# Attention on a graph: one more wait ahead of GpSimd's gathers, on VectorE's query product three steps back

## The reference, cut to what matters

```python
Q = (x @ Wq + bq).reshape(n, H, DH)
K = (x @ Wk + bk).reshape(n, H, DH)
V = (x @ Wv + bv).reshape(n, H, DH)
score = jnp.sum(K[src] * Q[dst], axis=-1) / np.sqrt(DH)
score = jnp.exp(jnp.clip(score, -5.0, 5.0))
wV = jax.ops.segment_sum(V[src] * score[..., None], dst, num_segments=n)
z = jax.ops.segment_sum(score, dst, num_segments=n)
attn = (wV / (z[..., None] + 0.001)).reshape(n, D)
h = layer_norm(x + attn, gamma1, beta1)
h = h + jax.nn.relu(layer_norm(h, gamma2, beta2) @ Wo + bo)
```

## Time and profile before

| | us |
|---|---|
| median of 3 runs | 2628.74 |
| lowest, highest | 2619.01, 2636.85 |
| the profiled execution's own time | 2645.04 |
| its span, first to last instruction | 2639.7 |
| first to last gather of attention (starts) | 1244.9 to 2591.6 |
| GpSimd busy with the 808 gather instructions | 786.8 |
| VectorE's 202 query products | 139.3, idle 715.9 before them |

### The profile page before, as it was taken

One profiled execution on the slowest core, in us unless ns is written; L12 is line 12 of the kernel. 1 busy time (PEld: TensorE's weight loads), 2 busy tenths in 40 slices (PEclk: granted clock), 3 DMA queues, 4 the chain that ended last, 5 costly groups with the idle time before them and its releaser, 6 DMA issues.

```text
span 2639.7 us, 44819 instructions
## 1 busy us (share of the span) xinstructions
PE 1717.0 (65%) x10229; PEld 1152.3 (44%) x10229; DVE 1372.1 (52%) x3608; ACT 937.1 (35%) x2332; POOL 1180.4 (45%) x1458
## 2 busy tenths in 40 slices
PE   2666666898989999897445555555555555554454
PEld 0222223454556565564344444444444444443443
DVE  8888876335656333365344444444454444444444
ACT  2777764234644222121132232232232322322223
POOL 4444434123534100012656565556555565555551
PEclk9555555899999999998666676666666666667666
DMA  1000001001111110134333333333333333333331
GB/s 66 0 0 0 0 10 50 23 28 43 54 51 57 31 32 29 29 97 135 112 99 113 95 118 99 101 104 112 94 111 98 107 118 95 108 110 98 104 96 32
DMA packets 148865, 188.64 MB, mean 71 GB/s; under 512 B 25795, under 2 KB 117316, under 8 KB 148804
## 3 DMA queue, kind: packets, MB, share of 16 engines
q0 software_dynamic: 38784, 105.96, 13.9%
q1 hardware_dynamic: 110020, 82.00, 9.9%
HBM read 162.82 MB, written 25.04 MB: 71 GB/s over the span
## 4 chain that ended last, share of the span: by engine, by line
another core or an unknown queue 17%; DVE 12%; issue 11%; PE 11%; ACT 1%; DMA 0%; POOL 0%; DVEq 0%; ACTq 0%
PE acc_bank L1391 5%; PE aq_bank L1372 4%; DVE counts L1497 3%; DVE a_score L1500 3%; DVE counts L1505 1%; PE ap_bank L1378 1%; DVE counts L1429 1%; DVE a_clipped L1510 1%; PE ac_bank L1408 0%; PE ac_bank L1407 0%; DVE counts L1453 0%; DVE a_stat L1460 0%; POOL counts L1302 0%; DVE counts L1446 0%
## 5 line engine op out<-in xcount | busy, mean ns | idle before, releaser
L1302 POOL DMA_INDIRECT counts<-keys_values,a_index x808 | 786.8, 974 | 564.9 <-ACT a_index L1317 336.0
L813 PE MATMUL z_bank<-y_parts,counts 128*128 128x384 bf16 (+1 forms) x3750 | 666.5, 329 | 4.1 <-DMA y_parts<-in_L_gnn_bq 4.1
L1497 DVE TENSOR_TENSOR counts<-aq_bank,counts 128x512 f32<-128x512 f32 x202 | 139.3, 690 | 715.9 <-remote 511.5
L1391 PE MATMUL acc_bank<-counts 128*128 128x136 f32 x1616 | 347.4, 370 | 236.6 <-issue 132.7
L1372 PE MATMUL aq_bank<-counts 128*128 128x128 bf16 x2424 | 285.0, 263 | 329.6 <-issue 314.0
L813 PEld LDWEIGHTS z_bank<-y_parts,counts 128*128 (+1 forms) x3750 | 370.2, 99 | 239.0 <-issue 15.0
L1391 PEld LDWEIGHTS acc_bank<-counts 128*128 128x128 f32 x1616 | 293.4, 260 | 278.2 <-issue 152.5
L1372 PEld LDWEIGHTS aq_bank<-counts 128*128 128x128 bf16 x2424 | 212.0, 120 | 387.6 <-issue 378.6
L1333 ACT ACTIVATE counts<-a_clipped 128x32 f32<-128x32 f32 x202 | 46.1, 228 | 896.3 <-DVE a_clipped L1510 780.1
L381 POOL TENSOR_TENSOR key_low_build<-iota_b_build,src_cols_build 128x768 bf16<-128x768 bf16 x102 | 151.7, 1488 | 210.6 <-DVE flat_build L452 196.4
L469 DVE TENSOR_TENSOR counts<-share_build,counts 128x300 f32 x408 | 166.3, 468 | 42.1 <-PE share_build L533 40.8
(11 more groups left out here) (159 smaller groups left out, 2061.0 us busy)
## 6 DMA issues: line engine op xcount, KB each, us to landing
counts<-group_rel_rows SPq DMA_DIRECT2D x34, 768.0 KB
counts<-keys_values,a_index POOLq DMA_INDIRECT x808
self_term<-s_out SPq DMA_DIRECT2D x150, 64.0 KB, 1.6
s_in<-self_term SPq DMA_DIRECT2D x150, 64.0 KB, 1.8
residual<-x_in SPq DMA_DIRECT2D x75, 64.0 KB, 1.6
counts<-query_parts SPq DMA_DIRECT2D x34, 96.0 KB
x_in<-in_x SPq DMA_DIRECT2D x50, 64.0 KB, 1.8
x_in<-residual SPq DMA_DIRECT2D x50, 64.0 KB, 1.9
```

The costliest lines, as they stand in the source:

```text
L813: yield s, nc.tensor.matmul(bank(p, dt)[:, 0:width], counts[:, bass.ds(dt.value(P) + s * NA, P)], y3[(p - 1) % 2][:, s, 0:width], start=s ...
L1302: nc.gpsimd.indirect_dma_start(rows_kv[:, j, c, :], None, v.kv, bass.IndirectOffsetOnAxis(index[:, j, c:c + 1], 0)).then_inc(gathered[j], 16)
L1391: ins = nc.tensor.matmul(acc_bank[ga.slot()][:, 0:TW], pick[:, s2.slot(3), c, :], msg[:, s2.slot(3), c, :], start=j == 2 and c == 0, stop= ...
L1497: nc.vector.tensor_tensor(prod[:, :].rearrange("p (c d) -> p c d", c=GC), q_bank[s.slot()][:, :].rearrange("p (c d) -> p c d", c=GC), rows ...
```

## The change

Ahead of a step's four gathers GpSimd gets a third wait. Beside the row numbers and the free slot, gather s now waits for s-2 query products, which is for the product of step s-3. The two other waits stay. No instruction moves on any engine; each step from s = 3 on gets one wait (with the increment of `held` that follows each such wait). The first three steps have none.

```diff
     RG = GS
+    LEAD_OF_GATHERS = 3
     PAIR = 2 * GS
...
                 if sub(s):
                     (s + 1).count(pool, index_ready, held)
                     (s - (RG - 1)).count(pool, msg_done, held)
+                    (s - (LEAD_OF_GATHERS - 1)).count(pool, prod_done, held)
                     for c in range(GC):
                         nc.gpsimd.indirect_dma_start(rows_kv[:, j, c, :], None, v.kv,
                                                      bass.IndirectOffsetOnAxis(index[:, j, c:c + 1], 0)).then_inc(gathered[j], 16)
```

## The result

The changed kernel takes 2559.99 us (median of 4 runs, 2556.61 to 2563.45) against 2626.59 us of the kernel before: a ratio of 0.9718, 95% interval 0.9693 to 0.9743. It is faster by 2.8%, where 1% slower was forecast; rival A had put it at 2569 us.

What follows compares the result with a forecast made beforehand. No engine is full; an order of events paces attention's gathers, with TensorE slow while they run. Gathers +31 us and the end -6.5 give +25 us, taking the median of 2628.74 to 2654; range 2580 to 2700.

Steps and rivals of the forecast that it cites:

- rival A: Attention's gathers: the third product's matmuls still get out, so all cycles have three steps; -60 us, 2569 us; chance 0.18.
- Point 1: GpSimd's waits before each step's gathers: the new wait on product s-3 is always the last to end.
- Point 2: GpSimd's gathers: released by the product itself, a run starts at 1.67 us in place of 3.92, 2.25 us sooner.
- restart: VectorE: the first query product after a run of gathers; its start is the time T that the forecast counts from.
- Point 3: GpSimd: a run's first gather meets VectorE's message product and costs 0.25 us more a run, ends 0 and 0.5.
- Point 4: TensorE: the third product's query matmuls end 3.6 to 3.9 us into the run, past 3.3; most cycles pass only two.
- Point 5: Gather cycles: 14.25 us for two steps, 19.25 for three, 3 in 10 of three; 6.85 us a step.
- rival C: Attention's gathers: a third product never passes, 7.12 us a step in place of 6.67; +79 us, 2708 us; chance 0.15.
- Point 6: Gathered rows: with two or three products a cycle they are there at the restart, so their lateness costs nothing.
- Point 7: The sum: gathers 1378 us against 1346.7, +31; the stage's end 9.2 us in place of 15.7, -6.5; together +25.
- Rival B: TensorE isn't held by the gathers, so the shorter pause is pure gain; -124 us, 2505 us; chance 0.06.
- the crawl: TensorE's results come out very slowly from soon after a run of gathers starts until its last rows have landed.

Runs made afterwards that it cites:

- qd3_c: Changed kernel with GpSimd's third wait on TensorE's query matmuls of step s-3 in place of VectorE's product: 2510.45 us against 2638.71 for the kernel before (0.9530).
- late3: Changed kernel with GpSimd's third wait on ScalarE's copy of the selection of step s-3 in place of VectorE's product: 2618.15 us against 2625.32 before (0.9963).
- lead4_c: Changed kernel with the third wait on the product of step s-4 in place of s-3: 2560.7 us against 2638.71 for the kernel before (0.9715).
- few_long: Changed kernel plus 4 matmuls of 512 columns ahead of each step's query matmuls, written over by them: 2552.18 us, ratio 0.9714 to the kernel before.
- many_short: Changed kernel plus 12 matmuls of one column ahead of each step's query matmuls, written over by them: 2557.52 us, ratio 0.9746 to the kernel before.
- direct_c: Changed kernel with GpSimd issuing plain DMAs of 1 KB rows from fixed places in place of indirect gathers: 1942.61 us, kernel before at 2638.71.
- half_rows: Changed kernel with gathers of 512 bytes a row in place of 1 KB, wrong rows and no values: 2311 us in three sets.
- after2: The changed kernel itself, unaltered, run again in another set: 2322.76 us against 2326.15 for the kernel before (0.9983).

## Why the prediction was wrong

It was wrong at the fourth step ("what is late next"), and the price of the fifth was too high. The others stand:

- Point 1, the new wait is the last one: right. 221.7 us of the pauses, 73 times, end on the product.
- Point 2, the run starts 1.67 us after the restart: 1.50 measured, the median over the runs (3.92 before).
- Point 3, the first gather made longer by the message product: right, 1.33 us in the median where 1.2 to 1.5 was forecast. All gathers together became 33 us longer; 22 was reckoned, 0 to 44 were the ends. In qd3_c, whose run starts ahead of the message product, the first gather takes 0.94 us.
- Point 4: wrong. The third product's query matmuls were to end 3.6 to 3.9 us into the run, and so to be caught in seven cycles of ten. They ended at +4.03, later still, and were caught in hardly any: 54 of 59 third products came promptly. I took the limit as a time from the run's start (3.3 us, a few up to 4.3). The kernel before can't tell this from a limit counted from the restart, since its runs nearly all start at one distance from it. The changed kernel can: of all query matmuls that ended 3.5 to 5.5 us after the run's start, 5 of 48 had a prompt product before and 53 of 59 after.

The table has the third product of each cycle of two steps and more. Prompt means that it started within 1.5 us of the end of its query matmuls and of VectorE's instruction before it. Times are medians; the instructions are TensorE's matmuls and weight loads on record from the restart to the end of those query matmuls.

| | run's start after restart, us | query matmuls' end after restart, us | instructions | prompt |
|---|---|---|---|---|
| before | 3.92 | 5.54 | 52 | 57 of 58 |
| late3 | 3.66 | 5.55 | 57 | 57 of 57 |
| after | 1.50 | 5.53 | 66 | 54 of 59 |
| lead4_c | 1.50 | 5.53 | 66 | 56 of 56 |
| few_long | 1.50 | 6.98 | 88 | 39 of 64 |
| many_short | 1.50 | 5.85 | 104 | 26 of 65 |
| qd3_c | 0.77 | 5.53 | 59 | 17 of 71 |

In the first four the matmuls end at the same distance from the restart and pass, wherever the run starts from 1.50 us on. So moving the run from 3.92 to 1.50 us costs hardly a product. The last three rows forbid a general limit in time from the restart: many_short's end 0.3 us later and mostly fail, few_long's end later than those and pass more often, and qd3_c's end at the same 5.53 us and mostly fail. A number of instructions since the restart, some 90, would fit all rows but qd3_c's. So the step that failed is known; what the limit is counted in is not.

- Point 5: the price of a cycle of three was right, 19.25 us forecast and 19.01 measured in the mean. Against the kernel before this gains 1.2 us a cycle and not the whole 2.25 of point 2: before, these cycles ran from 17.6 to 21.3 us with a mean of 20.20, and I took one of 21.25 for all. The share was wrong with point 4: of 69 runs 42 have three steps, 13 have more and 6 have two, in place of seven in ten with two. And the price of a cycle of two was too high: 14.25 us forecast, 13.4 in the only two of the changed kernel, 12.2 in many_short and 12.1 in qd3_c. Part of it is the 3.60 us from the last gather to the restart, read from one cycle: the kernel before's median is 3.16. At 6.1 us a step even cycles of two would have been faster than the 6.67 before, so rival C's slowdown wasn't there either. The stage takes 6.30 us a step, 6.85 was forecast and 6.42 was rival A's.
- Point 6, the rows come in time: right, VectorE waited for rows 5 times, 9.3 us.
- Point 7: the end of the stage gave 11.5 us, 6.5 was reckoned. The last product starts 4.2 us after the last gather, where 9.2 was put.

Rival A is what happened: the third product passes and the pause is simply shorter. It forecast 60 us, and the medians show 69 from 2628.74. The range of 2580 to 2700 was said to take in most of A and of C, and left out the times of both, 2569 and 2708.

Rival B has a share too. It took a rule, that DMA never contends with a compute engine (the Trainium skill, SBUF — State Buffer, section Who interferes with whom), to mean that the gathers don't hold TensorE. In three sets of five they don't: the kernel before takes 2326 us and the gathers run without a pause. In the sets with the crawl B fails: between 2136 and 2140 TensorE started nothing, and its signal came when the rows had stopped. Whether that goes against the rule isn't shown. direct_c moved rows at 214 GB/s with no product held, which agrees with it; what holds TensorE needn't be the transfer of rows.

What stays open: what the crawl is, what sets its limit, and why a whole set of runs has it or not. The number of the chip isn't the reason: the first set, with the crawl, and the second, without it, both have chip 14 on record. One thing was seen and not explained: the three sets that held half_rows had no crawl, and the two sets and the first measurement that didn't hold it had it. That it was about chance was my expectation before the fifth set; with that set it is six out of six, and no run tests it apart.

## What to carry to other kernels

Where an engine stops and restarts in cycles, ask for every threshold what it is counted from: a time from the one event, from the other, or a number of instructions. A trace with one rhythm can't tell them apart, and a forecast across the change then rests on a choice; look for a second kernel or stage in which they lie at different distances. Look at the cycles beside the time: two kernels with the same time (the changed one and many_short) had quite different ones. With the crawl it paid to release the long-running queue (GpSimd's gathers here) from the earliest event of the cycle that proves progress: by way of ScalarE 2618 to 2639 us, by VectorE's product 2560, by TensorE's matmuls 2510. Without the crawl it gives next to nothing: the kernel before takes 2326 and those by way of VectorE or TensorE 2323. And measure the kernel before beside each trial: here it moved by 300 us between sets, over four times what the change gains.

## What the runs showed of the hardware

The same kernel takes 2625 to 2639 us in some sets of runs and 2326 us in others, within 1% inside each. The difference is in the stage with indirect gathers: the changed kernel takes 237 us less in after2, and its gathers' starts span 1040.7 us in place of 1273.4. With plain DMAs of 1 KB rows from GpSimd instead, of 0.575 us each in the mean and always of the same 512 rows, the program takes 1940 us in a set without the crawl and 1943 in one with it. Indirect gathers of half the bytes keep their price: 970 ns each in half_rows, 985 in after2, both without the crawl.

A gather that starts while VectorE's message product runs is longer: the first of a run takes 1.33 us in the median of the changed kernel, where it starts inside that product, and 0.94 us in qd3_c, where it starts ahead of it.

```profile
L1304 POOL DMA_INDIRECT counts<-keys_values,a_index x808 | 783.5, 970 | 250.1 <-issue 226.5
```
